# Where a gather's wait stands in VectorE's program: six gates instead of four in a graph attention kernel

## The reference, cut to what matters

```python
kj = k[src] + e                                   # e = eattr @ We
alpha = sum(q[dst] * kj) / sqrt(C)
m = segment_max(alpha, dst)
a = exp(alpha - m[dst])
vj = v[src] + e
out = segment_sum(a * vj, dst) / segment_sum(a, dst) + x @ Ws + bs
```

## Time and profile before

| | us |
|---|---|
| median of 3 runs | 9136.32 |
| lowest and highest | 9121.11 and 9146.65 |
| profiled execution | 9139.4 |
| its span, first to last instruction | 9137.7 |
| VectorE busy | 4467.0 |
| GpSimd busy | 4947.5 |
| TensorE matmuls busy | 4442.9 |

### The profile page before, as it was taken

One profiled execution on the slowest core, in us unless ns is written; L12 is line 12 of the kernel. 1 busy time (PEld: TensorE's weight loads), 2 busy tenths in 40 slices (PEclk: granted clock), 3 DMA queues, 4 the chain that ended last, 5 costly groups with the idle time before them and its releaser, 6 DMA issues. The chain is left out here.

```text
span 9137.7 us, 150515 instructions
## 1 busy us (share of the span) xinstructions
PE 4442.9 (49%) x36670; PEld 3422.0 (37%) x36670; DVE 4467.0 (49%) x15728; ACT 974.7 (11%) x4096; POOL 4947.5 (54%) x5118
## 2 busy tenths in 40 slices
PE   7964444444444445444444444445444444444444
PEld 5753333333333334333333333334333333333333
DVE  6554444444444444444444444444444444444445
ACT  2220000000000001000000000001000000000000
POOL 2225555555555544555555555553555555555554
PEclk9975555555555555555555555555555555555555
DMA  5532222222222222222222222222222222222222
GB/s 132 159 100 69 69 68 71 70 70 68 70 68 71 69 64 72 71 68 70 71 71 69 71 69 70 71 68 71 69 70 69 73 68 71 70 70 69 70 70 60
DMA packets 687685, 675.81 MB, mean 74 GB/s; under 512 B 369235, under 2 KB 506389, under 8 KB 687637
## 3 DMA queue, kind: packets, MB, share of 16 engines
q0 software_dynamic: 161600, 320.52, 14.4%
q1 hardware_dynamic: 496944, 301.76, 12.4%
q10 hardware_dynamic: 29092, 52.97, 2.0%
HBM read 652.96 MB, written 21.67 MB: 74 GB/s over the span
## 5 line engine op out<-in xcount | busy, mean ns | idle before, releaser
L1333 POOL DMA_INDIRECT Gall<-KV,sdn x4848 | 4799.7, 990 | 3578.0 <-DVE OTs L717 1618.5
L901 PE MATMUL pS<-ident,Fs 16*128 16x16 f32 (+1 forms) x606 | 151.6, 250 | 3052.0 <-DVE Fs L767 2864.8
L706 DVE SCALAR_TENSOR_TENSOR O<-sdn,bf,iof 128x336 f32<-128x336 int32 x808 | 456.1, 564 | 2142.0 <-remote 2021.5
L901 PEld LDWEIGHTS pS<-ident,Fs 16*128 16x128 f32 (+1 forms) x606 | 106.9, 176 | 3468.7 <-issue 3468.7
L928 PE MATMUL pG<-O,vals 128*66 128x42 f32 (+1 forms) x10784 | 1297.0, 308 | 4.4 <-issue 3.7
L928 PEld LDWEIGHTS pG<-O,vals 128*66 128x66 f32 (+1 forms) x10784 | 1206.0, 223 | 51.0 <-ACT vals L965 27.1
L864 PE MATMUL pE<-bd,ea 128*128 128x256 f32 x1212 | 739.7, 714 | 13.1 <-PEq L971 12.6
L748 DVE TENSOR_TENSOR kj<-kj,pQ 128x512 f32<-128x512 f32 x606 | 416.9, 688 | 491.4 <-remote 438.6
L914 PE MATMUL pY<-fw,Ob 128*42 128x6 bf16 (+1 forms) x4848 | 257.7, 176 | 817.2 <-DVE cr L790 572.5
L869 PE MATMUL pE<-bd,ea 128*128 128x256 f32 x1212 | 642.8, 634 | 0.0
L950 ACT ACTIVATE fb<-df 42x64 f32<-42x64 f32 x606 | 154.7, 255 | 3974.9 <-DVE X L793 1497.8
(11 more groups left out here) (177 smaller groups left out, 6303.8 us busy)
## 6 DMA issues: line engine op xcount, KB each, us to landing
db<-D SPq DMA_DIRECT2D x606, 256.0 KB
ea<-in_ea SPq DMA_DIRECT2D x606, 128.0 KB
Gall<-KV,sdn POOLq DMA_INDIRECT x4848
db<-D ACTq DMA_DIRECT2D x202, 256.0 KB, 3.7
qw<-QT SPq DMA_DIRECT2D x1818, 5.2 KB
dr<-in_dr SPq DMA_DIRECT2D x1212, 4.0 KB
ea<-in_ea SPq DMA_DIRECT2D x202, 64.0 KB, 3.6
sdn<-in_sdn SPq DMA_DIRECT2D x606, 12.0 KB
```

Of the source, the lines that this page charges most:

```text
L706: return e.scalar_tensor_tensor(O[u][:, :, :], sdn[u][:, T:2 * T].unsqueeze(2).to_broadcast([128, T, W]), bf[:, bass.ds(s.value(), 1)], io ...
L1333: e.indirect_dma_start(G[u][:, j, :], None, kvtab, bass.IndirectOffsetOnAxis(ap=sdn[u][:, j:j + 1], axis=0)).then_inc(s_g[u], 16)
```

## The change

The table of gates has six entries in place of four, and other operations in it. A pass's first ten steps (four before) are unrolled, and each of them behind the third has one wait only, ahead of its first gather, for the operation that frees the buffer. The loop begins two rounds later. The lower bound of the number of rounds that is told to the compiler is the number of blocks; it emits no work.

```diff
-            return e.value_load(ntr[0:1, 0:1], min_val=1, max_val=(SM - 3 - z.peel) // 3)
+            return e.value_load(ntr[0:1, 0:1], min_val=(B - 3 - z.peel) // 3, max_val=(SM - 3 - z.peel) // 3)
...
-        gates = {0: ("acc", 4), 2: ("vals", 3), 4: ("vj", 1), 6: ("Mlo", 2)}
+        gates = {0: ("facc", 4), 1: ("OT", 1), 2: ("cr", 2), 5: ("vj", 1), 6: ("alpha", 1), 7: ("flag", 1)}
+
+        AHEAD = 2
...
             for j in range(T):
-                if j in gates and not fresh(s):
+                if isinstance(s.i, int):
+                    if j == 0 and not fresh(s):
+                        after(e, "V", "vj", s - 3)
+                        hold(e)
+                elif j in gates:
                     op, behind = gates[j]
                     after(e, "V", op, s - behind)
                     hold(e)
...
-            for c in range(3 + z.peel):
+            for c in range(3 * AHEAD + 3 + z.peel):
                 gathers(e, At(0, c))
-            with e.Fori(0, n) as i:
+            with e.Fori(AHEAD, n) as i:
                 for c in range(3 + z.peel, 6 + z.peel):
                     gathers(e, At(i, c))
```

## The result

The changed kernel took 9188.17 us (median of 6 runs, 9166.57 to 9214.72), the kernel before 9136.28 us in the same comparison (6 runs, 9121.11 to 9151.41). The ratio is 1.0056, with a 95% interval of 1.0041 to 1.0072: slower by 52 us, where I had forecast 60 us less. The profiled execution after took 9185.1 us with a span of 9183.4, which is 45.7 us over the span before.

A forecast was written before the change was run, and what follows sets the result against it. It took a loop of waits (run of gathers, late TensorE count, gate, next run) as the bound; 9139.4 - 60 + 0 = 9079 us, less 3 us to the median: 9076 us, 0.7% faster, range 8650 to 9310 us.

The forecast's parts named there:

- The bound and the loop of waits: Attention passes: run of gathers, late TensorE count, d1 to acc, gate, next run; common step 13.74 us, POOL idle 3.65.
- The 0.78 us from gate to gather: POOL, when idle: time from the end of a gate's operation to the start of the gather it holds, 0.78 us.
- Part 1: Common step, stalled at O (401 of 606): five new gates hold nothing, facc's nominal 0.24 us is lost; taken as 0.
- Part 2: Steps stalled at prod, 105 POOL idle times: seventh gather's gate opens earlier, by alpha not Mlo; 60 us gained.
- The 0.57 us: Steps stalled at prod: alpha ends 0.57 us ahead of Mlo, so the seventh gather starts that much earlier; counted 105 times.
- the rival "no change": Steps stalled at prod: the 0.57 us are given back at fhi's wait, time stays at 9136 us; chance 0.20.
- Part 3: First ten steps of a pass, 21 steps with one earlier gate: between 79 us gained and 20 us lost; taken as 0.
- the slower side: Common step: first gather 0.24 us closer to OT and vals upsets the step, 9236 to 9308 us; chance 0.30.
- The broken runs by cr: Third gather's gate cuts the run when fhi stalls, so counts come sooner: 8350 to 9000 us; chance 0.18.

The follow-up runs named there:

- n2: Kernel before with its second gather held until vj of the previous step and the third gather's gate dropped: 8721.63 us beside 9029.70, ratio 0.9656.
- m1: Kernel before, with d1 also waiting until all eight gathers of the run in progress have landed: 9280.50 us, ratio 1.0293.
- m2: Changed kernel with the old short unrolled part, and d1 also waiting until the run's eight gathers have landed: 9304.13 us, ratio 1.0318.
- e1: Changed kernel with the short unrolled part of the kernel before: 9043.62 us, ratio 1.0035 with late counts; ratio 0.9999 without.
- m3: Changed kernel, with d1 also waiting until its step's eight gathers have landed: 9340.14 us, ratio 1.0357.
- e2: Changed kernel with the old table of four gates in the loop: 9075.89 us, ratio 1.0074 with late counts; ratio 0.9981 without.
- e4: Changed kernel, but each first step's one wait is for facc, one iteration later: 9053.53 us, ratio 1.0052 with late counts; ratio 1.0000 without.
- n1: Kernel before, with SyncE waiting for d1 of step s-4, not flag of step s-3, ahead of a step's loads: 9081.12 us, ratio 1.0049.

## Why the prediction was wrong, step by step

**The bound and the loop of waits**: right for the chips with late counts. Run, late count, d1, gate, run is what every trace of that kind shows. That it holds whenever gathers are dense was wrong: the same kernel took 7072 us on one chip, and 9024 us on that chip some minutes later.

**The 0.78 us from gate to gather**: right; it holds behind alpha in the changed kernel and behind vj in n2.

**Part 1, the common step**: the step was right (13.80 us, first gather of 1.57 us, nothing gained from facc). The cost of 0 for the two additional waits was wrong in one kind of step. In every thirteenth step POOL pauses behind the first gather, and with the new table the pause is 0.24 us longer. These steps took 12.39 us before and 12.83 after (mean of 42), so 45 of them make 20 us. The table cost 24 us between m1 and m2 and 0.35% in e1. I placed the gates on the common step only, and never on this one.

**Part 2, the other pattern**: this is the first of two steps of the prediction that failed, and the sign of the forecast hung on it, as its 60 us were the only term that wasn't 0. The 0.57 us came as computed in single steps (12.41 us), but I multiplied it by all 105, as if an earlier run changed nothing else. Consecutive steps of the pattern took 13.10 us before and 13.29 after, and the stalls at prod rose from 101 to 149. A run that starts earlier meets fhi's count at its edge, as the rival "no change" said; the rows show that in one pair of steps. e1 shows the sum of parts 1 and 2 as a loss of 28 us of median time, where I had a gain of 60. Leaving out the second largest wait, that of d1 (869.9 us), hid how easily a stall moves from one operation to the next.

**Part 3, the first ten steps**: this is the second step that failed, and it makes most of the measured loss. It bounded the effect between 79 us gained and 20 us lost, named the mechanism of the loss (sixteen gathers in one go), and then took 0, because it leaned on a gain of which no row showed anything. The mechanism is what happened, and it was mis-sized: two steps take 32.9 us and not 29.4. The last gather of the long run began at 696.27 and VectorE was released at 700.29, 4.0 us later and not 2.6, which is 1.4 of the 3.5 us. Measured: 40 us by the traces, 36 us by m3 against m2, 0.74% in e2.

**The sum**: head 36 to 40 us, gates 24 to 28, together 60 to 68, where the changed kernel lost 52 (37 to 66 by its interval). Its own trace has 40 us in the first twelve steps of the passes and 11 behind them. So the head is sure, and the loop's gates cost something between 0 (e1 against e2 by their traces) and 28 us. e2's 67 us (47 to 86 by its interval) are more than its head shows (39 us over three passes by its trace), and why is open; single runs of the kernel before differ by up to 54 us on that chip, perhaps as steps fall into one pattern or the other.

**The rivals**: the slower side was right, by another mechanism than the one that I gave it. No common step of 14.0 to 14.2 us appeared. The Trainium skill (SBUF — State Buffer, Who interferes with whom) would have the instruction that issues first hold the port pair and the other one block. The row after doesn't bear the rival out: the gather began at 4063.59, 0.08 us ahead of vals, and it was the gather that took 1.57 us, while vals kept its 0.67. Nor does it refute the rule, since OT ran from 4063.29 to 4063.74 and so issued ahead of both. The broken runs by cr didn't come: in the common step nothing waits ahead of the third gather.

**What would make it wrong**: I had written that it fails if the lateness depends on how far POOL has issued ahead. The changed kernel, m3 and e4 show that it depends on how long the run of gathers goes on (runs of eight against sixteen); what in the chip delays a semaphore's count beside gathers, and why one chip had it in one set of runs and not in another, wasn't found. SyncE's issues aren't needed for it (n1).

## What to carry to other kernels

A wait that no trace ties to its producer is a condition of its own: find out whether it is always there before you sum with it, by the kernel's time on another chip. Where counts come late in the tail of a dense run of gathers, what pays is not fewer or earlier gates but a start of the run at which its tail lies beside a wait for data (n2, 3.4% faster on the one chip that ran it); an earlier gate can make the run longer and the lateness with it. A gain of one operation's wait is only worth its count times its length if no other stall of the loop can take its place. And a bound that has a mechanism in the rows outweighs one that has only arithmetic: between them, 0 is not the middle.

## What the runs showed of the hardware that I had not expected

- The same kernel takes 7072 us or 9015 to 9136 us. In the second case TensorE's counts and SyncE's instructions are late while gathers run densely, in the first they aren't, with gathers of the same 0.95 us and the same 0.30 between them. One chip showed both some minutes apart.
- The lateness is not a fixed delay. Behind eight gathers it was 5.8 us, and behind sixteen 18.8 us.
- Every thirteenth step, 104 gathers apart, POOL pauses between the first and the second gather, in every trace with late counts (2.99 us from one to the other in m1, where 1.65 is common). The traces without late counts show no such pause.
